# A filtered leaky ReLU kernel on TensorE: two of the eight up steps of the loop body go from 64 by 64 tiles to 64 by 128

## The reference

```python
lin = jnp.einsum('oc,chw->ohw', W, coord) + b[:, None, None]
x = x + jnp.sin(lin)[None]                      # (2, 512, 256, 256)
out = x + bias[None, :, None, None]
out = upfirdn(out, up_filter * 2, up=2)         # along columns, then rows: 512 x 512
out = leaky_relu(out, 0.2) * sqrt(2)
out = upfirdn(out, down_filter, down=2)         # back to 256 x 256
```

## Time and profile before

| | |
|---|---|
| median of 3 runs | 5984.38 us (5983.77 to 5988.2) |
| the profiled execution | 5984.24 us, span 5981.9 us |
| mean granted TensorE clock | 0.997 |
| TensorE matmul busy | 5888.6 us, 98% of the span |
| VectorE, ScalarE, GpSimd busy | 68%, 72%, 22% |
| matmul and weight load records | 294912 each |

### The profile page before, as it was taken

One profiled execution on the slowest core, in us unless ns is written; L12 is line 12 of the kernel. 1 busy time (PEld: TensorE's weight loads), 2 busy tenths in 40 slices (PEclk: granted clock), 3 DMA queues, 4 the chain that ended last, 5 costly groups with the idle time before them and its releaser, 6 DMA issues.

```text
span 5981.9 us, 667608 instructions
## 1 busy us (share of the span) xinstructions
PE 5888.6 (98%) x294912; PEld 5770.6 (96%) x294912; DVE 4069.0 (68%) x7231; ACT 4290.9 (72%) x9222; POOL 1307.8 (22%) x1034
## 2 busy tenths in 40 slices
PE   5999999999999999999999999999999999999998
PEld 5999999999999999999999999999999999999998
DVE  5666666666666666666666666666666666666665
ACT  4777777777777777777777777777777777777776
POOL 1222222222222222222222222222222222222221
PEclk9999999999999999999999999999999999999999
DMA  2344334333344344344344344344344443444342
GB/s 82 114 114 114 114 114 114 114 114 114 114 114 114 114 114 114 114 114 114 114 114 114 114 114 114 114 114 114 114 114 114 114 115 114 114 115 114 114 114 87
DMA packets 632632, 673.74 MB, mean 113 GB/s; under 512 B 41888, under 2 KB 566176, under 8 KB 632608
## 3 DMA queue, kind: packets, MB, share of 16 engines
q1 hardware_dynamic: 632608, 673.37, 39.5%
HBM read 403.72 MB, written 269.48 MB: 113 GB/s over the span
## 4 chain that ended last, share of the span: by engine, by line
PE 98%; issue 1%; DVE 1%; DMA 0%; ACT 0%; SPq 0%; ACTq 0%; DVEq 0%
PE p_ps L457 34%; PE a_ps L457 33%; PE y_ps L457 32%; DMA bias_wide<-in_L_conv_bias_dram 0%; DVE up_band L369 0%; DMA f_rows<-trig_dram 0%; DVE angle L329 0%; DVE angle L330 0%; ACT trig L244 0%; DMA trig_dram<-trig 0%; DVE down_band L371 0%; DVE angle_rows L330 0%; DVE angle_rows L329 0%; DVE phase L340 0%; DVE turns L328 0%
## 5 line engine op out<-in xcount | busy, mean ns | idle before, releaser
L390 DVE SCALAR_TENSOR_TENSOR z<-y_ps,leak 128x512 f32<-128x512 f32 x4096 | 2683.0, 687 | 1416.6 <-ACT leak L265 1416.4
L457 PE MATMUL y_ps<-up_band,a_sb 64*64 64x138 f32 (+2 forms) x65536 | 2852.2, 279 | 4.1 <-issue 3.2
L457 PEld LDWEIGHTS p_ps<-down_band,z 64*64 64x64 f32 x131072 | 2264.9, 135 | 137.3 <-issue 137.2
L457 PE MATMUL p_ps<-down_band,z 64*64 64x40 f32 (+1 forms) x131072 | 2326.7, 224 | 23.8 <-issue 9.2
L231 POOL TENSOR_TENSOR x_sum<-x_raw,f_sb 128x512 f32<-128x512 f32 x1024 | 1306.0, 1275 | 4625.7 <-DVE f_sb L407 3853.6
L265 ACT ACTIVATE leak<-y_ps 128x512 f32<-128x512 f32 x4096 | 2254.2, 611 | 3.9 <-PE y_ps L457 3.5
L457 PEld LDWEIGHTS y_ps<-up_band,a_sb 64*64 64x64 f32 x65536 | 2104.6, 133 | 5.6 <-issue 5.6
L271 ACT COPY o_out<-a_ps 128x256 f32<-128x256 f32 x2048 | 662.1, 375 | 1287.0 <-PE a_ps L457 1287.0
L457 PE MATMUL a_ps<-up_band,x_sum 64*64 64x138 f32 (+2 forms) x32768 | 1420.0, 280 | 54.4 <-POOL x_sum L231 50.0
L457 PE MATMUL a_ps<-down_band,p_rows 64*64 64x40 f32 (+1 forms) x65536 | 1388.6, 223 | 7.7 <-issue 6.1
L457 PEld LDWEIGHTS a_ps<-down_band,p_rows 64*64 64x64 f32 x65536 | 1297.2, 135 | 8.5 <-issue 8.5
(11 more groups left out here) (29 smaller groups left out, 31.3 us busy)
## 6 DMA issues: line engine op xcount, KB each, us to landing
x_raw<-in_x_dram SPq DMA_DIRECT2D x1024, 256.0 KB, 3.2
out_dram<-o_out SPq DMA_DIRECT2D x1024, 256.0 KB, 2.2
f_rows<-trig_dram SPq DMA_DIRECT2D x512, 256.0 KB, 4.0
trig_dram<-trig SPq DMA_DIRECT2D x4, 256.0 KB, 2.0
w_wide<-in_L_conv_W_dram SPq DMA_DIRECT2D x1, 512.0 KB, 4.6
b_wide<-in_L_conv_b_dram SPq DMA_DIRECT2D x1, 256.0 KB, 5.1
bias_wide<-in_L_conv_bias_dram SPq DMA_DIRECT2D x1, 256.0 KB, 5.6
up_taps<-in_L_conv_up_filter_dram SPq DMA_DIRECT2D x1, 6.0 KB, 2.3
```

What stands on the lines that cost most here:

```text
L390: nc.vector.scalar_tensor_tensor(z[n][:, i, :], y_ps[i][:, :], GAIN, leak[i % 2][:, :], ALU.mult, ALU.max).then_inc(z_done, 1)
L457: last = nc.tensor.matmul(outs[o][half * HALF:(half + 1) * HALF, lo:hi], data[row, where[k], col:col + HALF], band[row, start:start + hi - ...
```

## The change

A new function `wide_step` does an up step in tiles of 64 rows by 128 columns: the loop over half is gone, and each call takes 128 columns of data as weights and writes 128 partitions of the bank. It has 4 calls where step_of has 8, with the same columns of the band, the same banks and the same sums. `up_rows` and `up_cols` use it for step 1 when `wide` is set, `ups` hands it on, and only the last call of the loop body sets it. The semaphore waits and increments stay as they are.

```diff
+            def wide_step(outs, data, at, step):
+
+                pe.sem_inc(steps_begun, 1)
+                for k in range(HT):
+                    for rows in range(2):
+                        o = rows ^ step
+                        row = slice(rows * HALF, (rows + 1) * HALF)
+                        lo, hi, start = UP_SPAN[k][rows]
+                        last = nc.tensor.matmul(outs[o][:, lo:hi], data[row, k, (at + o) * P:(at + o + 1) * P],
+                                                up_band[row, start:start + hi - lo], start=step == 0 and k == 0,
+                                                stop=step == 1 and k == HT - 1, skip_group_check=True)
+                return last
...
             def up_rows(m, n, step, first=False, wide=False):
...
                     pe.wait_ge(a_half, m + 1)
+                    if wide:
+                        wide_step(a_ps, x_sum[n], 0, 1).then_inc(a_made, 1)
+                        return
...
             def up_cols(m, n, pair, step, wide=False):
...
                     pe.wait_ge(y_half, 2 * m + pair + 1)
+                    if wide:
+                        wide_step(outs, a_sb[n], 2 * pair, 1).then_inc(y_made, 2)
+                        return
...
                 if a_next:
-                    up_rows(m + 1, 1 - n, 1)
+                    up_rows(m + 1, 1 - n, 1, wide=wide)
                 if y:
-                    up_cols(m, n, 0, 1)
+                    up_cols(m, n, 0, 1, wide)
...
                 ups(c, 1)
                 downs(c, 1)
-                ups(c + 1, 0)
+                ups(c + 1, 0, wide=True)
```

More of the change, by code:

```diff
@@ L462, in step_of, with up_rows @@
                 return last
-            def up_rows(m, n, step, first=False):
+            def up_rows(m, n, step, first=False, wide=False):
                 if step == 0:
@@ L474, in up_rows, with up_cols @@
                     pe.wait_ge(a_half, m + 1)
+                    if wide:
+                        wide_step(a_ps, x_sum[n], 0, 1).then_inc(a_made, 1)
+                        return
                     step_of(a_ps, x_sum[n], up_band, UP_SPAN, 0, range(HT), range(HT), 1, True).then_inc(a_made, 1)
-            def up_cols(m, n, pair, step):
+            def up_cols(m, n, pair, step, wide=False):
                 outs = y_ps[2 * pair:2 * pair + 2]
@@ L517, in down_cols, with ups @@
                             (0, 2, 1, 3), range(UT), 1, True).then_inc(o_made, 1)
-            def ups(c, n, a_next=True, y=True, first=False):
+            def ups(c, n, a_next=True, y=True, first=False, wide=False):
                 m = 2 * c + n
```

## The result

The changed kernel took 6038.88 us in the median of 6 runs (6036.44 to 6044.65), the kernel before 5988.11 us in the median of 6 beside them: ratio 1.0085, 95% interval 1.0075 to 1.0095. It is slower by 51 us, about half of the 111 us that were forecast (6095 against 5984). The profiled run has a span of 6034.5 us, 52.6 more than before.

The account below looks back on a forecast made before the run. TensorE, busy 98% of the span, was taken as the bound. Two shape switches, less what the hole hides, add 0.22 us in 508 passes, 112 us: 5984.2 to 6095 us; range 5955 to 6135, forecast's own 6060 to 6135.

Parts of the forecast that it names:

- the old hole: TensorE's idle 0.249 us in each of the 508 loop passes, before the first p_ps load at the loop's end.
- The place of the hole and the sequencer's chain behind it: At the loop's end a sequencer chain from the y_half wait, about 0.17 us then 0.72 us, outlasts TensorE's steps.
- Streaming unchanged: Each of the last two up steps of a pass stays 0.46 us, four matmuls per tile at 0.115 us.
- Loads hidden: In the wide steps, 128-column loads of 57.5 to 115 ns hide behind matmuls: 0 added, at most 0.92 us a pass.
- Rival 3: Loads in the wide steps are not hidden: up to 0.92 us a pass, 6450 us, some 6560 with switches; chance 0.03.
- The switch: Tile shape changes before the a_ps step and back before p_ps: 0.25 us each, bounds 0 and 0.38 us.
- The reason for the switch: At the shape change, a 128-column load fills two tiles where the previous step's matmuls are in flight; no separate size.
- The sequencer's saving: In the loop's last step, 16 fewer instructions save at most 0.06 us a pass, but the chain is overtaken: worth nothing.
- rival 1: Both shape changes are cheap, at most 0.115 us each: 15 to 30 us less, 5954 to 5969 us; chance 0.25.
- rival 2: Both shape changes cost 0.12 to 0.16 us each, cancelling the instruction saving: 5972 to 5996 us; chance 0.11.
- Rival 4: Both shape changes cost 0.38 us each: 234 us more, 6218 us; chance 0.04 together with everything above 6135.
- What rides along: a_made, the VectorE and ScalarE copies and GpSimd's x_sum come about 0.22 us later in each pass; their slack stays.

## Why the prediction was right or wrong

The direction and the mechanism held: slower, through two switches of shape, with the old hole hiding the larger part of their cost. The size was off by half. Point by point:

- **The place of the hole and the sequencer's chain behind it: right.** One wait less shortened it by 0.13 us a pass and brought 68 us; another place of the cut made it longer (0.37 in place of 0.25 us).
- **Streaming unchanged: right.** Behind a wide step that is not the first, the next stands 0.46 us later (the run with four wide steps). The prediction's sign for it, 0.46 us between the two wide steps, did not come: it is 0.56, by the exposed load of the first.
- **Loads hidden: right in a run of wide steps.** The reason given was circular, since the 0.115 us of a matmul was itself a quarter of the step's 0.46 us; it holds because steps with loads of 64 and of 128 columns both keep 0.46 us. Rival 3 does not occur. For the one load that is exposed the prediction named 0.057 us on top of its sum; the first matmuls stand 0.106 us longer.
- **The switch, the term that was mis-sized.** The prediction let the new load start "when the last matmul's record ends" and put the matmul 0.03 us behind it. Measured, at both switches the load starts 0.07 us before that end. At the first switch the error was made good, by luck, by something that I had left outside the sum: the exposed load of 128 columns, 0.10 us, so -0.07 + 0.10 is the 0.03 that I had put there, and the first switch does cost 0.25 us. At the second the load has 64 columns, and the matmul stands at 0.07 before the record's end and not 0.03 after it: 0.10 us a pass too much, 508 x 0.10 = 51 us. The sum was 1.16 to 1.20 us from the record's end to p_ps, the trace has 1.05. Its lower end is 0.11 too much, and the 0.22 that I took lies 0.01 above the difference of that end: 508 x 0.12 = 61 us, and 112 less 61 is the 51 that were measured.
- **The reason for the switch: wrong.** That the load reaches over two tiles in use is not needed: a load that fits into one old tile waits as well (the tiles of 64 by 32).
- **The sequencer's saving: overtaken, as said, and at the lower end of what was said.** From the wait within 3004.12 to 3004.14 to the loop's counter within 3004.27 to 3004.29 it is 0.15 us, against 0.17 with 32 instructions: 0.02 us, not 0.03 to 0.06. In the run with four wide steps, where this chain does end last, it takes 0.82 us from that wait to the first load, in the kernel before 0.87 in the mean of all passes (0.84 to 0.89), that is 0.043 us less (0.866 and 0.822). Had the switches been free, the saving would have brought an estimated 10 to 22 us (508 x 0.02 to 0.043), against the 15 to 30 of rival 1.
- **The ranges.** 6039 us lies in the wide range and below the forecast's own (6060 to 6135), between rival 2's upper end of 5996 and that. What was missing was a case for a switch of about 0.2 us. The bounds were 0, 0.25 and 0.38, and the start of the next load before the modelled end of a record was not thought of, though it was known from the profile that these ends are modelled. Rival 4's sum also takes 0.15 us where its bound is 0.16, which changes its time by 5 us and no conclusion.
- **What rides along: right.** The copies and the sum that wait for a_made start later with the rest (copies of a_ps and sum after 0.72, 0.65 and 1.68 us of idle time, before 0.52, 0.46 and 1.49), and TensorE has no wait for them in the loop.

## What to carry to other kernels

A change of TensorE's tile shape between two steps has a price each way, here 0.25 us into the wider shape behind a step of long matmuls, 0.15 us behind one of short matmuls, and 0.12 us back where nothing covers it, while the step in the new shape cost nothing by itself: gather the steps of one shape, and put the switch behind short matmuls or where TensorE waits anyway. Half as many instructions help only where the sequencer is what ends last, and there a redundant wait behind the branch was worth far more (68 us for one line) than 16 instructions (0.02 to 0.04 us a pass). When a hole is to be filled with a new cost, compare the cost with the hole in distances between the starts of steps: the listed waits fell here while the kernel became slower.

## What the runs showed of the hardware that was not expected

- At a change of tile shape the next load started 0.07 us before the end of the last matmul's record wherever nothing later held it (the changed kernel: 71 to 72 ns in all 508 passes at both switches), for 128, 64 and 32 columns, and behind records of 275 and of 226 ns.
- The first load behind a switch into a wider or narrower shape is exposed: the first matmul stood 106 ns longer with 128 columns and 26 ns with 32.
- A TensorE loop body of four units in place of two took 1.88 times as long, with 41.89 MB on the instruction queue in place of 0.36 and a granted clock of 0.85. Where the limit lies between the two bodies was not measured.
- The sequencer passes 32 instructions of a step in 0.12 us, but a step of 64 behind another of 64 in 0.51 us.
